# Normalized x of the first layer moved from tile to tile in stripes of four tokens, and its 32x32 transpose placed two reductions into the turn

## The reference, cut to what matters

```python
def first_layer(x, emb, mask, ...):
    xn = layer_norm(x, norm_w, norm_b)
    q = (xn @ q_w + q_b).reshape(B, T, 16, 16); k = (xn @ k_w + k_b).reshape(...)
    att = softmax(einsum('bnhl,bmhl->bnmh', q, k) + mask terms, axis=2)
    y = einsum('bnmh,bmhl->bnhl', att, xn @ v_w + v_b)
    h = layer_norm(y, ...) * (1 + scale) + shift      # scale, shift from emb
    return x + silu(h) @ out_w + out_b
```

## Time and profile before

| | us |
|---|---|
| median of 3 runs | 867.61 (867.24 to 867.9) |
| the profiled execution, its own time | 869.6 |
| its span, first to last instruction | 867.8 |
| mean granted clock of TensorE | 0.994 |

### The profile page before, as it was taken

The page is one execution under the profiler, slowest core; times in us unless marked ns, Lnnn a source line. Parts: engine busy times, 40 slices in busy tenths (PEclk is TensorE's granted clock), DMA queues, the critical chain, the costliest instruction groups (busy, mean ns, idle before and its releaser), DMA issues.

```text
span 867.8 us, 23658 instructions
## 1 busy us (share of the span) xinstructions
PE 832.3 (96%) x8092; PEld 686.9 (79%) x8092; DVE 773.2 (89%) x1590; ACT 679.0 (78%) x1208; POOL 679.9 (78%) x1165
## 2 busy tenths in 40 slices
PE   4999999999999999999999988999999999999996
PEld 4777777777777777777777656899999999999996
DVE  6689999999998999999998967899999999999976
ACT  2247777777777777777778796899999999999975
POOL 3375878878888888888786337899999999999965
PEclk9899999999999999999999999999999999999999
DMA  8854665565656565655654424345454444444311
GB/s 258 263 175 165 198 219 187 207 209 191 220 183 212 179 222 181 221 196 196 219 178 164 142 64 107 96 126 144 152 149 143 136 142 140 138 150 141 116 31 62
DMA packets 129847, 143.69 MB, mean 166 GB/s; under 512 B 13312, under 2 KB 85984, under 8 KB 129600
## 3 DMA queue, kind: packets, MB, share of 16 engines
q1 hardware_dynamic: 129728, 142.19, 50.5%
HBM read 49.50 MB, written 38.11 MB: 101 GB/s over the span
## 4 chain that ended last, share of the span: by engine, by line
PE 77%; DVE 13%; issue 6%; POOL 1%; ACT 1%; SPq 1%; DMA 0%; DVEq 0%; ACTq 0%; POOLq 0%
PE psY L1721 12%; PE psX L1600 11%; PE psT L1600 10%; PE psM L1600 10%; DVE sb_cm L1158 6%; PE psT L1700 5%; PE psY L1600 5%; PE psT L1679 4%; PE psT L1883 3%; PE psY L1836 3%; PE psT L1611 3%; PE psM L1700 3%; PE psY L1746 2%; DVE sb_xF L1172 2%; PE psM L1679 2%
## 5 line engine op out<-in xcount | busy, mean ns | idle before, releaser
L1158 DVE TENSOR_REDUCE sb_cm<-psT 128x4 f32<-128x1024 f32 x168 | 202.8, 1213 | 20.5 <-PE psT L1700 20.3
L741 ACT ACTIVATE sb_P<-psT 128x1024 f32<-128x1024 f32 x176 | 177.8, 1026 | 42.6 <-PE psY L1721 23.5
L1721 PE MATMUL psY<-sb_P,sb_Vp 128*17 128x256 f32 x2048 | 129.4, 381 | 1.9 <-DVE sb_yr L1193 1.2
L1158 DVE TENSOR_REDUCE sb_cm<-psM 128x4 f32<-128x1024 f32 x88 | 106.7, 1213 | 11.5 <-PE psM L1700 11.5
L741 ACT ACTIVATE sb_P<-psM 128x1024 f32<-128x1024 f32 x80 | 82.0, 1025 | 21.6 <-PE psY L1721 11.7
L1600 PE MATMUL psX<-sb_xT,sb_W0h 128*128 128x256 f32 x488 | 93.6, 294 | 0.0
L1721 PEld LDWEIGHTS psY<-sb_P,sb_Vp 128*17 128x17 f32 x2048 | 50.3, 97 | 46.8 <-DVE sb_yr L1193 1.9
L521 POOL TENSOR_TENSOR sb_qp<-sb_qp 128x512 fp32r<-128x512 f32 x64 | 82.3, 1285 | 5.3
L1700 PE MATMUL psT<-sb_Ks,sb_Qs 64*128 64x256 f32 x672 | 76.6, 310 | 2.6 <-DVE sb_cm L1158 2.5
L1679 PE MATMUL psT<-sb_Qs,sb_Ks 64*128 64x256 f32 x704 | 75.5, 298 | 1.6 <-ACT sb_P L741 1.4
L1600 PEld LDWEIGHTS psX<-sb_xT,sb_W0h 128*128 128x128 f32 x488 | 71.4, 192 | 4.6 <-ACT sb_qp L764 0.2
(11 more groups left out here) (215 smaller groups left out, 2553.4 us busy)
## 6 DMA issues: line engine op xcount, KB each, us to landing
sb_Qs<-sb_qp SPq DMA_DIRECT2D x96, 256.0 KB
sb_Ks<-sb_qp SPq DMA_DIRECT2D x96, 256.0 KB
sb_xt<-in_x SPq DMA_DIRECT2D x32, 256.0 KB, 3.4
y_normed<-sb_Yn SPq DMA_DIRECT2D x32, 256.0 KB, 2.7
sb_u<-y_normed SPq DMA_DIRECT2D x128, 64.0 KB, 2.6
out<-sb_v SPq DMA_DIRECT2D x31, 256.0 KB, 2.4
x_biased<-sb_xo SPq DMA_DIRECT2D x28, 256.0 KB, 2.3
sb_u<-x_biased SPq DMA_DIRECT2D x28, 256.0 KB, 3.3
```

Of the source, the lines that this page charges most:

```text
L741: a.activation(P[G % 4][:, :], pairs[place["S", n, g][0]][:, :], ACT.Exp).then_inc(s_ex, 1)
L1158: v.tensor_reduce(cm[n % 2][:, 4 * j:4 * j + 4], scores, AX.X, ALU.max, negate=True).then_inc(s_mx, 1)
L1721: ins = pe.matmul(psY[32 * j:32 * j + 17, y0:y0 + T], Vp[n % RING][:, m, 4 * gr + j, :], Pj[:, c0:c0 + 256], start=(m == 0), stop=(m == 1))
```

## The change

The DRAM tensor and the store go away. `nblocks` copies `xs` straight into `xB` by four DMAs between on-chip tiles, one for each column group. The source is 128 partitions of 128 elements and the destination 32 partitions of 512 elements, and both are walked in the same order, so four consecutive source partitions (tokens 4s to 4s+3) fill one destination partition 32a+s. Hence the block b of a partition now holds token 4s+b where it held token 32b+s, and the DVE transpose writes its output in another order: the 32 elements of a block go to `xF` at a step of four elements instead of side by side.

Two things move. On SP the four DMAs stand where the store stood, ahead of `parts(t, 0)` (behind `parts(t, 1)` for sample 6, as before). On DVE `xturn(t+1)` stands behind `maxima(t, 1)` for t = 6 to 30, and in its old place for t = 5. POOL's `xnorm` now waits for the four copies of the sample before, where it waited for the store.

```diff
-            def nstore(n):
+            def nblocks(n):
+
                 sp.wait_ge(s_xn, n + 1)
-                sp.dma_start(xnd[n], xs[:, :, :, :, :].rearrange("p a i k c -> p (a i k c)")).then_inc(s_nd, 16)
-
-            def nblocks(n):
-
-                sp.wait_ge(s_nd, 16 * (n - BY_BLOCK + 1))
                 if n > BY_BLOCK:
                     sp.wait_ge(s_xf, n - BY_BLOCK)
-                by_block = xnd[n].rearrange("(b s) (a e) -> a s b e", s=32, a=4)
-                tile = xB[:, :, :].rearrange("p k t -> p (k t)").rearrange("p (b e) -> p b e", b=4)
-                for q in range(4):
-                    sp.dma_start(tile[32 * q:32 * q + 32, :, :], by_block[q]).then_inc(s_nb, 16)
+                tile = xB[:, :, :].rearrange("p k t -> p (k t)")
+                for a in range(4):
+                    sp.dma_start(tile[32 * a:32 * a + 32, :], xs[:, a, :, :, :].rearrange("p i k c -> p (i k c)"))\
+                        .then_inc(s_nb, 16)
...
                 if ok(t + 2) and t + 2 > BY_BLOCK:
-                    nstore(t + 2)
+                    nblocks(t + 2)
...
                 if t + 2 == BY_BLOCK:
-                    nstore(t + 2)
-                if ok(t + 2) and t + 2 >= BY_BLOCK:
                     nblocks(t + 2)
...
                 if n > BY_BLOCK:
-                    g.wait_ge(s_nd, 16 * (n - BY_BLOCK))
+                    g.wait_ge(s_nb, 64 * (n - BY_BLOCK))
...
-                v.transpose(xF[:, :, :].rearrange("p i t -> p (i t)").rearrange("p (q b s) -> p b q s", q=4, b=4),
+                v.transpose(xF[:, :, :].rearrange("p i t -> p (i t)").rearrange("p (q s b) -> p b q s", q=4, b=4),
...
                 maxima(t, 1)
+                if BY_BLOCK < t + 1 < B:
+                    xturn(t + 1)
...
                 maxima(t, 5)
-                if t + 1 >= BY_BLOCK and ok(t + 1):
+                if t + 1 == BY_BLOCK:
                     xturn(t + 1)
```

More of the change, by code:

```diff
@@ L93, in bass_cond_seq_kernel @@
     fd = nc.dram_tensor("y_second", (B, 128, 2 * D), F32, kind="Internal").ap()
-    xnd = nc.dram_tensor("x_normed", (B, 128, 2 * D), F32, kind="Internal").ap()
     yd = nc.dram_tensor("y_normed", (B, 128, 2 * D), F32, kind="Internal").ap()
@@ L227, in bass_cond_seq_kernel @@
         s_ws, s_wh, s_woh = sem("s_ws"), sem("s_wh"), sem("s_woh")
-        s_nd, s_nb, s_xf = sem("s_nd"), sem("s_nb"), sem("s_xf")
+        s_nb, s_xf = sem("s_nb"), sem("s_xf")
         s_lw = [sem(f"s_lw{i}") for i in range(3)]
```

## The result

| | before | changed kernel |
|---|---|---|
| median, us | 867.52 (867.24 to 867.9, 4 runs) | 880.73 (876.64 to 883.14, 4 runs) |
| profiled execution, its own time and its span | 869.6, 867.8 | 882.85, 881.1 |
| mean granted clock | 0.994 | 0.992 |
| ratio | | 1.0147, 95% interval 1.0102 to 1.0193 |

The account below looks back on a forecast made before the run. PE and DVE holding each other up were taken to pace the 14.95 us turn. A turn of 14.80 + 0.25 = 15.05 adds 2.5 us in 25 turns, less 0.3 once: +2.2, median 869.8 us, range 861 to 877.5.

Parts of the forecast that it names:

- What is queued behind them on SP: On SP, the four copies shift those of q and k by 1.0 to 2.1 us, within a slack of 2.3.
- Rival 4: SP becomes the bound: issues of 1.0 us each, shift 3.7, k 1.4 late, 0.5 a turn, 880 us; chance 0.06.
- loop over two turns: From PE's first row maxima through division, `ynorm` and next-but-one `xnorm`; some 2.9 us of slack against late k.
- The sum of the turn: Whole turn: 14.80 + 0.25 = 15.05 us, 0.10 longer, +2.5 us in 25 turns.
- Putting it into the new place: Transpose behind `maxima(t, 1)` closes a loop through POOL's `xlow`, `ynorm` and `csplit`: 14.80 us, gain 0.15 a turn.
- Taking the transpose off the old place: DVE's division starts earlier; the loop through `maxima(t, 1)` and first `yturn` becomes 14.65 us, alone gaining 0.30 a turn.
- The transpose's own price: DVE transpose writing at a 16-byte step costs 0.25 us more, 0.95 in all; bounds nothing to +0.53.
- DVE row: Profiled DVE reduction with innermost step of 32 elements, 0.49 ns more per element: +0.25 us for the transpose.
- POOL row: Profiled POOL memset at a step of 17 elements, 0.8 ns more per element: +0.43 us for the transpose.
- Rival 2: Strided write of the transpose costs 0.43 to 0.53; at 0.5 a turn lasts 15.30, 876.1 us; chance 0.14.
- The transfer: Removing store and DRAM round trip is worth nothing itself; copies land by 321.5, the transpose comes at about 321.6.
- POOL's idle time before `csplit`: Sign on POOL: its idle 0.38 us a turn is eaten by the loop through `xlow` and must be gone.

Follow-up runs that it names:

- e3: Changed kernel with the zero and mask row DMAs issued ahead of SP's wait for `xnorm`; 873.94 us, ratio 1.0061.
- e4: Changed kernel with early zero and mask DMAs and contiguous write, true token order kept by permuted loads and store of x; 865.03 us, ratio 0.9965.
- e11: e7 with the copy of the shift rows also issued ahead of the wait for `xnorm`; 865.38 us, ratio 0.9940.
- e7: e4 with the transpose moved from behind `maxima(t, 1)` to behind `ystats(t-5, 1)`; 866.41 us, ratio 0.9981.
- e1: Kernel before with only the transpose's write made strided (every fourth element), true token order left out; 877.02 us, ratio 1.0096.
- e10: e4 with the copy of the shift rows also issued ahead of the wait for `xnorm`; 865.15 us, ratio 0.9947.
- e9: Changed kernel with contiguous write, transpose in its old place, zero and mask DMAs early, true token order left out; 869.43 us, ratio 0.9999.
- e12: e11 with the change's strided write and plain loads of x; 870.98 us, ratio 1.0012.
- e8: e4 with the transpose moved behind `maxima(t, 3)`; 873.34 us, ratio 1.0061.
- e2: Changed kernel with the transpose's write made contiguous again, true token order left out; 881.12 us, ratio 1.0136.

## Why the prediction was wrong

The step that failed is **"What is queued behind them on SP"**. It put the shift at 1.0 to 2.1 us, the landing of k's last copy at 324.8 and R5 at 327.10, and said: "The slack of 2.3 takes a shift of 2.1. This is the cover, and it is nearly used up". The size of the shift was right: from 4.79 us in the turn read to 2.6 to 2.7 in the middle ones. Wrong was to take one landing and one distance from one turn as those of every turn, and so to put PE's wait at R5 at nothing; it measured 13.5 us. Both vary. The issue of 322.31 and its end at 324.8 make 2.5 us, and k is indeed there by 2.6 or 2.7 in most turns; but in four of the 25 turns R5 can't start until 4.24 to 4.72 us behind the issue (6.7 us of waits), and in six others, where k is there after 2.6 to 3.2 us, PE gets there 1.4 to 2.4 us behind it (4.8 us). The other 2.1 us lie in five turns between the two. Before, a landing of 4.72 would still have been within 4.79 and left no mark in the waits; that is why nothing in the profile spoke of it. Two of the waits also cost more than their length, since the granted clock fell behind them. Rival 4, "SP becomes the bound", had the right place and the right time (880 us), and by the prediction's own sign (PE waiting at R5 for a DMA) it is the one that came true. The time was luck: it rests on issues of 1.0 us, a shift of 3.7 and a loss in every turn. The four issues took 2.51 us (2.4 were taken), and ten of the 25 turns have no wait at all. Its loop over two turns, from a late R5 to a late issue of k, would fit the issue at 194.08, but no run takes it apart. I gave it 0.06.

**The sum of the turn** came out: 15.05 predicted, 15.06 to 15.08 measured in turns without a wait (e3 and the changed kernel).

```profile
360.32 1.27 POOL L489 TENSOR_TENSOR sb_xT<-sb_xF,sb_xT 128x512 fp32r<-128x512 f32 x1
375.40 1.29 POOL L489 TENSOR_TENSOR sb_xT<-sb_xF,sb_xT 128x512 fp32r<-128x512 f32 x1
390.49 1.28 POOL L489 TENSOR_TENSOR sb_xT<-sb_xF,sb_xT 128x512 fp32r<-128x512 f32 x1
```

Its terms did so in part by luck. **"Putting it into the new place"**, 14.80: 14.77 measured in e4. **"Taking the transpose off the old place"**, 14.65: 14.65 in e11 and e7, where PE's own list takes as long. **"The transpose's own price"**, 0.25: mis-sized. Its working also has a slip: (1.21 - 0.69) / 512 is 1.02 ns per element and not 1.04, which makes a contiguous 128 take 296 ns and the price 0.21 by the DVE row. The instruction grew by 0.42, the value of the POOL row (0.43) and not that of the DVE row; but its neighbours hide some of it, so that 0.30 arrives in the turn. The rule of the Trainium skill, page "Advanced Engine Details and Errata", section "SBUF Cachelines", that a pattern with fewer than two hits on a 16-byte line pays a penalty, agrees with e1: one hit a line, 1.11 for 0.70 us. Rival 2's instruction came true, at 0.3 a turn instead of its 0.5.

**"The transfer"**: the landing "without much to spare" was right as a warning and priced at nothing; the waits of DVE that end with it are 1.8 us in the changed kernel, 5.5 in e3, 5.4 in e10. That the removal of the DRAM way is worth nothing by itself is shown by e9 (0.9999). POOL's idle time before `csplit`, 10.8 us in 27 waits before, is 1.7 in 8 now, as the forecast wanted to see.

The account of +13.6 us in the 25 turns: waits for the copies of k and what hangs on them, 388.0 - 378.9 = +9.1 (e3); write step, 378.9 - 371.5 = +7.4 (e4 against e3); new place, 371.5 - 374.4 = -2.9 (e4 against before). The last is less than the 25 x 0.18 = 4.5 of the loops and the 1.6 between them fits with DVE's waits for xB copies in e4 (3.8 us in 4 turns), some of which only replaces the wait for POOL; that part is argued. The forecast had only the last two terms, and its +2.2 us stands against 7.4 - 2.9 = 4.5 there.

Still open: what makes a landing late (the instruction packets were only seen beside it), what makes the distance from issue to R5 vary, and the tenth of a microsecond in e12's transpose.

## What to carry to other kernels

A DMA's cover has to be held against the slowest landing, and the smallest distance, not against those that one turn shows: look at the distance from issue to first use in every turn, and count a change that eats 2 of 4.8 us as a risk even where no wait is in the profile. On an in-order issuing queue, first move what needs no fresh data ahead of the wait, then put new issues in; here that was worth 9 us once the copies were there and nothing before. A place that looks free on one engine has to be followed to the next: in e8 and e12 the transpose stood ahead of a reduction that PE wanted. And a gain in a loop is only worth measuring once each of the change's side costs is taken away by itself: e2 removed one of two and saw nothing.

## What the runs showed of the hardware

- A DVE block transpose of 128x512 float32 takes 0.70 us with a contiguous write, and 1.10 to 1.14 when it writes at a step of 16 bytes; 1.22 in the place of e12.
- The 256 KB store of `x_biased`, issued right behind the last copy of k in the changed kernel, landed after 4.2 to 4.7 us in the nine turns with a packet of the instruction queue 0.5 to 3 us behind that copy's issue, and after 2.7 to 3.1 in the sixteen without. PE's wait for k was long only where the packet came within 1.5 us, or where PE itself was early.
- Waits of PE of 1.84 and 1.76 us were followed by some 5 us with a granted clock of 0.62 to 0.70; those of 1.60 and 1.53 us were not.
